# Selective scan and attention, two passes on one core: VectorE's side jobs moved to other engines in the first pass, the rotation and the position terms rebuilt in the second

## What is computed

```python
x = x + _L0_conv_ref(_gn(x), ...)   # state-space block
x = x + _L1_conv_ref(_gn(x), ...)   # attention block

# _L0: xh, z = split(x @ in_proj_w.T); xc = silu(conv3x3(xh) + conv_b)
#      four directions k: dts, Bs, Cs from x_proj_w; dts = softplus(dts @ dt_projs_w + bias)
def step(h, inp):                    # 192 channels x 16 states x 4 directions, 1024 steps
    u_t, d_t, B_t, C_t = inp
    dA = jnp.exp(d_t[..., None] * As)
    h = h * dA + (d_t * u_t)[..., None] * B_t[:, :, None, :]
    y = jnp.einsum('bkcn,bkn->bkc', h, C_t)
#      y summed over directions, layer norm, times silu(z), @ out_proj_w.T

# _L1: q, k, v = x @ w_qkv + b; 12 heads of 32
def rot(t):                          # pairs (even, odd) turned by cos, sin of the position
    return stack([t0 * c - t1 * s, t0 * s + t1 * c], axis=-1)
attn = einsum(rot(q), rot(k)) * scale
attn = attn + rel_h[..., :, None] + rel_w[..., None, :]   # q times a table, by row and by column
out = softmax(attn) @ v @ w_proj + b_proj
```

## Time and profile before

| | us |
|---|---|
| median of 3 runs | 3307.79 |
| lowest, highest | 3305.24, 3314.67 |
| profiled execution, its own time | 3309.41 |
| span of that execution in the trace | 3307.6 |
| busy: TensorE, VectorE, ScalarE, GpSimd | 2748.0, 2366.0, 1557.4, 1335.6 |

### The profile page before, as it was taken

The page is one execution under the profiler, slowest core; times in us unless marked ns, Lnnn a source line. Parts: engine busy times, 40 slices in busy tenths (PEclk is TensorE's granted clock), DMA queues, the critical chain, the costliest instruction groups (busy, mean ns, idle before and its releaser), DMA issues. The chain is left out here.

```text
span 3307.6 us, 40573 instructions
## 1 busy us (share of the span) xinstructions
PE 2748.0 (83%) x15824; PEld 1382.7 (42%) x15824; DVE 2366.0 (72%) x2262; ACT 1557.4 (47%) x1908; POOL 1335.6 (40%) x636
## 2 busy tenths in 40 slices
PE   3577777887678876777667999989998999989999
PEld 1222223332233332222222665556554665555655
DVE  1598899999999999999982466625664356625665
ACT  4445644555435564444431356514563346514564
POOL 4478766887668876766651100011000200011000
PEclk8789998999999999999896999999999999999999
DMA  1334443355443544445541111020111110020110
GB/s 61 128 115 133 153 144 141 130 140 159 145 149 127 140 159 145 161 134 144 182 137 60 30 33 52 1 71 1 33 52 40 33 33 25 29 71 1 33 52 20
DMA packets 93429, 297.51 MB, mean 90 GB/s; under 512 B 15804, under 2 KB 18504, under 8 KB 93224
## 3 DMA queue, kind: packets, MB, share of 16 engines
q1 hardware_dynamic: 93224, 294.73, 28.6%
HBM read 238.57 MB, written 23.07 MB: 79 GB/s over the span
## 5 line engine op out<-in xcount | busy, mean ns | idle before, releaser
L1608 POOL TENSOR_TENSOR arena<-arena 128x1024 f32<-128x1024 f32 x384 | 902.9, 2365 | 325.9 <-DVE arena L1092 277.3
L1092 DVE TENSOR_TENSOR_SCAN arena<-PS,arena 128x1024 f32<-128x1024 f32 x384 | 878.2, 2287 | 86.1 <-ACT PS L1445 62.5
L1445 ACT ACTIVATE PS<-arena,a_inf,a_neg 128x1024 f32<-128x1024 f32 x384 | 463.8, 1208 | 776.8 <-DVE arena L1092 772.4
L564 PE MATMUL PS<-arena,ident 128*128 128x512 f32 x1568 | 804.1, 639 | 19.3 <-ACT arena L1456 15.1
L1225 DVE CUSTOM_DVE_ANT_1 arena<-PS,arena 128x1024 f32<-128x1024 f32 x384 | 467.6, 1219 | 350.4 <-PE PS L851 350.4
L1533 ACT ACTIVATE arena<-arena,neg_max 128x1024 f32<-128x1024 f32 x384 | 441.0, 1149 | 513.4 <-DVE neg_max L1225 513.4
L555 PE MATMUL PS<-arena,sel 96*128 96x512 bf16 x768 | 247.7, 406 | 413.0 <-DVE arena L1100 409.3
L1100 DVE TENSOR_TENSOR arena<-arena,PS 128x1024 f32<-128x1024 f32 x384 | 459.3, 1196 | 9.7 <-PE PS L555 8.9
L564 PEld LDWEIGHTS PS<-arena,ident 128*128 128x128 f32 x1568 | 318.5, 204 | 304.2 <-issue 246.9
L851 PE MATMUL PS<-arena 64*128 64x512 f32 x1536 | 433.1, 641 | 11.1 <-DMA arena<-arena 11.1
L862 PE MATMUL PS<-ident,arena 128*128 128x128 f32 x3072 | 413.9, 278 | 2.6 <-ACT arena L1533 2.6
(11 more groups left out here) (125 smaller groups left out, 2286.2 us busy)
## 6 DMA issues: line engine op xcount, KB each, us to landing
arena<-b_rows SPq DMA_DIRECT2D x256, 512.0 KB, 3.7
arena<-b_rows SPq DMA_DIRECT2D x256, 256.0 KB, 4.0
arena<-arena SPq DMA_DIRECT2D x192, 128.0 KB, 2.9
arena<-arena SPq DMA_DIRECT2D x120, 64.0 KB, 2.0
normed<-xn SPq DMA_DIRECT2D x5, 1536.0 KB, 6.4
normed<-x_in SPq DMA_DIRECT2D x4, 1536.0 KB, 7.9
residual<-x_in SPq DMA_DIRECT2D x4, 1536.0 KB, 8.0
x<-residual SPq DMA_DIRECT2D x4, 1536.0 KB, 6.4
```

What stands on the lines that cost most here:

```text
L564: last = pe.matmul(dst[:, half(h)], lhs, rhs[:, half(h)], start=start, stop=stop, skip_group_check=True)
L1092: dve.tensor_tensor_scan(HS[:, at % 2, ::step], DA[:, ::step], DBU[:, at % R3, ::step], 0.0, ALU.mult, ALU.add).then_inc(scan_done.sem, 1)
L1445: act.activation(DA, DELTA[:, tile % 2, :], ACT.Exp, bias=a_inf[:, col:col + 1], scale=a_neg[:, col:col + 1]).then_inc(da_ready.sem, 1)
L1608: pool.tensor_tensor(DBU[:, at % R3, :], DU[:, tile % 2, :], BSB[:, at % R3, :], ALU.mult).then_inc(dbu_ready.sem, 1)
```

## The change

First pass. The statistics, their moments, both norms, the addition of x, the mask and the split into bfloat16 parts leave VectorE. ScalarE takes the sums (activations with an accumulated output), the norms, the mask (one Relu into bytes; the activation `soft_third` goes), the casts; GpSimd takes small products and the two subtractions of the split; TensorE adds x by a third product with the identity. The next image's statistics and norm move into the previous image's items (negative places), many jobs are placed anew, and the first image's front products run on VectorE instead of GpSimd.

Second pass. The weights' columns are ordered so that a head's even and odd parts lie 64 rows apart: the rotation is two VectorE products from swapped halves, without `turn`. A head's rows are then gathered by 10 DMAs instead of 6. The row term comes out of `relh`, 16 products with 32-column weights per job, already by query; the column term takes the one-hot rows. `relw` and half of `rel` go.

```diff
-HEAD_DMAS = 6
+HEAD_DMAS = 10
-PE_MID = {("y", 0, 0): 7, ("y", 0, 1): 8, ("y", 0, 2): 9, ... ("out", 0): 42, ("out", 1): 43, ("out", 2): 44,
-          ("out", 3): 45, ("out", 4): 46, ("out", 5): 47, ("stats",): 53}
+PE_FRONT = {("stats",): -8, ("xh", 0): 5, ("xh", 1): 6, ("xh", 2): 7, ("pad", 0): 25.5, ("pad", 1): 26, ("pad", 2): 27,
+            ("z", 0, 0): 56, ("z", 0, 1): 57, ("z", 0, 2): 58, ("z", 1, 0): 61, ("z", 1, 1): 62, ("z", 1, 2): 63,
+            ("dts", 0): 70, ("dts", 1): 71, ("dts", 2): 72, ("bc", 0): 75, ("bc", 1): 76, ("bc", 2): 77}
+PE_MID = {("y", 0, 0): 9, ("y", 0, 1): 10, ("y", 0, 2): 11, ("y", 1, 0): 13, ("y", 1, 1): 14, ("mean", 0): 21,
+          ("mean", 1): 22, ("var", 0): 30, ("var", 1): 31, ("out", 0): 43, ("out", 1): 44, ("out", 2): 45,
+          ("out", 3): 46, ("out", 4): 47, ("out", 5): 48, ("stats",): 53}
-DVE_MID = {... ("add", 0): 44, ("add", 1): 45, ("add", 2): 46, ...
+DVE_MID = {("centre", 0): 24, ("centre", 1): 25, ("scale", 0): 34, ("scale", 1): 34.5}
+ACT_FRONT = {("stat", 0, 0): -20, ("stat", 0, 1): -19, ("stat", 1, 0): -18, ("stat", 1, 1): -15, ("stat", 2, 0): -14,
+             ("stat", 2, 1): -11, ("means",): -6, ("rstd",): -4, ("norm", 0): -3, ("norm", 1): -2, ("norm", 2): -1,
+             ("xh",): 8, ("pad",): 28, ("z", 0): 59.5, ("z", 1): 64.5,
+             ...
+             ("ucopy", 3): 69, ("dts",): 73.5, ("brows",): 79, ("bchi",): 80, ("bmid",): 83, ("blo",): 86}
+ACT_MID = {("yf", 0): 12, ("yf", 1): 16, ("sq", 0): 27, ("sq", 1): 28.5, ("rstd",): 33, ("affine", 0): 35.5,
+           ("affine", 1): 37, ("out", 0): 43.9, ("out", 1): 44.9, ("out", 2): 45.9, ("out", 3): 46.9, ("out", 4): 47.9,
+           ("out", 5): 48.9, ("means",): 54.9, ("rstd2",): 56, ("norm", 0): 58.9, ("norm", 1): 60.5, ("norm", 2): 61}
+POOL_FRONT = {("var",): -5.5, ("bias",): -3.5, ... ("rest", 0): 81.5, ("rest", 1): 85}
+def front_due(table, b, i):
...
+            item = at + ITEMS * (f - b - 1)
+            if f == 1 and at < 0:
+                item = (at + EARLY) * 0.2
...
                     half_product(banks(k % 2, 1), h, [
                         (W["w_out"][:, 0, c * P:(c + 1) * P], flat(yf(m, 0))),
-                        (W["w_out"][0:XT, 1, c * P:(c + 1) * P], flat(yf(m, 1)[0:XT, :]))]).then_inc(op_psum.sem, 1)
+                        (W["w_out"][0:XT, 1, c * P:(c + 1) * P], flat(yf(m, 1)[0:XT, :])),
+                        (idn, flat(X[:, c, :]))]).then_inc(op_psum.sem, 1)
...
+                elif what == "out":
+                    k, = args
+                    h, c = divmod(k, CT)
+                    act.wait_ge(op_psum.sem, op_psum.at(2 * CT * m + k + 1))
+                    act.activation(X[:, c, half(h)], banks(k % 2, 1), ACT.Copy, accum_out=half_sums[:, h, c, 0:1])
+                    act.activation(banks(k % 2, 1), banks(k % 2, 1), ACT.Square, scale=1.0 / IMG,
+                                   accum_out=half_sums[:, h, c, 1:2]).then_inc(x_saved.sem, 1)
...
+            def small_mask(tile):
+                act.activation(MASK, SE, ACT.Relu, bias=mask_top[:, 0:1], scale=-MASK_TOP / SMALL
+                               ).then_inc(soft_mask.sem, 1)
...
             def soft_series(tile):
-                dve.wait_ge(soft_e.sem, soft_e.at(tile + 1))
-                dve.tensor_scalar(MASK, SE, SMALL, None, ALU.is_lt)
                 dve.wait_ge(soft_q2.sem, soft_q2.at(tile + 1))
-                dve.scalar_tensor_tensor(out=SQ3, in0=SQ3, scalar=2.4375, in1=SE, op0=ALU.add,
+                dve.scalar_tensor_tensor(out=SQ3, in0=SQ3, scalar=0.8125, in1=SE, op0=ALU.add,
                                          op1=ALU.mult).then_inc(soft_q.sem, 1)
...
+        JOBS = [[("proj", n) for n in range(4)] + [("rel", 0), ("rel", 1), ("relh", 0), ("relh", 1)],
+                [("proj", n) for n in range(4, 10)] + [("rel", n) for n in range(2, 6)]
+                + [("relh", n) for n in range(2, 6)],
+                [("proj", 10), ("proj", 11)]]
+        JOB_AT = [{k: m for m, k in enumerate([2, 4, 6, 8, 10, 12, 16, 18, 20, 22, 24, 25, 26, 27])}, {6: 0, 10: 1}, {}]
...
+                    copies = [[], [], [(QX[2 * HD * h + HD:2 * HD * h + 2 * HD, j, :], RELC[j::HG, g // 2, :])
+                                       for h in range(2)]]
+                    for h in range(2):
+                        for odd in range(2):
+                            at = XT * odd + HALF_HEAD * j
+                            rows = slice(2 * HD * h + HALF_HEAD * odd, 2 * HD * h + HALF_HEAD * (odd + 1))
+                            copies[0].append((QX[rows, j, :], QKC[at:at + HALF_HEAD, PLACE[g, "q"], :]))
+                            copies[1].append((KX[rows, j, :], QKC[at:at + HALF_HEAD, PLACE[g, "k"], half(h)]))
...
+                        for r in range(IMG // 2):
+                            at = h * IMG // 2 + r
+                            t, row = divmod(r, HG)
+                            last = pe.matmul(dst[IMG * row:IMG * row + IMG, t * P:(t + 1) * P],
+                                             QKC[:, PLACE[g, "q"], at * IMG:(at + 1) * IMG],
+                                             W["rel_h"][:, 0, HG * (IMG - 1 - at):HG * (REL - at)],
+                                             start=True, stop=True, skip_group_check=True)
...
-                        dve.tensor_tensor(RT2[:, h, :], src, W["sin"][:, 0, half(h)], ALU.mult
+                        dve.tensor_tensor(RT2[0:XT, h, :], raw[XT:P, :], W["sin"][XT:P, 0, half(h)], ALU.mult)
+                        dve.tensor_tensor(RT2[XT:P, h, :], raw[0:XT, :], W["sin"][0:XT, 0, half(h)], ALU.mult
                                           ).then_inc(sin_done.sem, 1)
```

More of the change, by code:

```diff
@@ L49 @@
[L49 to L60, removed]
@@ L73, in due @@
-def due(table, i):
-    return sorted((job for job, at in table.items() if i <= at < i + 1), key=table.get)
+            POOL_FRONT[("add", _m, _j)] = _b
+SIG_ORDER = sorted(range(4), key=lambda which: ACT_FRONT[("sig", which, 0)])
+SIG_DONE = sorted(range(4), key=lambda which: ACT_FRONT[("sig", which, 2)])
+CAP_ORDER = sorted(range(4), key=lambda which: POOL_FRONT[("cap", which)])
+SP_FRONT = {("next_x",): 72, ("z_store",): 80, ("b_store",): 83, ("bcs",): 89}
+SP_MID = {("x_load",): 1, ("z_load",): 2, ("x1_store",): 52, ("xn2_store",): 67}
@@ L78, in in_order, with mid_due @@
 def in_order(table):
     return sorted(table, key=table.get)
+def front_due(table, b, i):
+    found = []
+    for job, at in table.items():
+        for f in (b + 1, b + 2):
+            item = at + ITEMS * (f - b - 1)
+            if f == 1 and at < 0:
+                item = (at + EARLY) * 0.2
+            if f < B and i <= item < i + 1:
+                found.append((item, f, job))
+    return [(f, job) for item, f, job in sorted(found, key=lambda found: found[0])]
+def mid_due(table, b, i):
+    return sorted((job for job, at in table.items() if b and i <= at < i + 1), key=table.get)
@@ L521, in _ @@
                         sp.wait_ge(s_psum.sem, s_psum.after(b, STEPS * g - HG + j + 1))
-                        for dst, src in operands(g, j):
+                        for dst, src in itertools.chain(*operands(g, j)):
                             sp.dma_start(dst, src).then_inc(head_loaded[j].sem, 16)
@@ L786, in value_product @@
                         last.then_inc(v_psum.sem, 1)
-                job_saved = {"proj": raw_saved, "turn": sin_done, "rel": rel_saved, "relw": relw_saved}
+                job_saved = {"proj": raw_saved, "rel": rel_saved, "relh": relh_saved}
                 def job(phase, m, blocks=()):
@@ L1101, in times_c @@
                                   ).then_inc(hc_ready.sem, 1)
-            for job in in_order(DVE_FRONT):
-                front(0, *job)
+            for job in in_order(POOL_FRONT):
+                if job[0] not in ("var", "bias"):
+                    front_products(dve, 0, *job)
             dve.wait_ge(consts.sem, consts.at(N_CONST))
@@ L1238, in _ @@
                     biased_scores(s)
-                    if k - 2 in JOB_AT[g]:
-                        job(g + 1, JOB_AT[g][k - 2])
+                    for after, kinds in ((4, ("proj",)), (2, ("rel", "relh"))):
+                        if k - after in JOB_AT[g] and JOBS[g + 1][JOB_AT[g][k - after]][0] in kinds:
+                            job(g + 1, JOB_AT[g][k - after])
                     if g + 1 == GROUPS and k - 2 in LATE_AT:
@@ L1705 @@
     mats["w_out"] = wo
-    mats["w_qkv"] = np.asarray(L1_conv_w_qkv)
+    pos = np.arange(P)
+    paired = HD * (pos % XT // HALF_HEAD) + 2 * (pos % HALF_HEAD) + pos // XT
+    qkv_order = np.arange(3 * C)
+    for k in range(2 * GROUPS):
+        qkv_order[k * P:(k + 1) * P] = k * P + paired
+    mats["w_qkv"] = np.asarray(L1_conv_w_qkv)[:, qkv_order]
     mats["w_proj"] = np.asarray(L1_conv_w_proj)
@@ L1718 @@
     mats["to_high"] = np.eye(P, k=XT)
-    turn = np.zeros((P, P), f)
-    for i in range(0, P, 2):
-        turn[i + 1, i] = -1.0
-        turn[i, i + 1] = 1.0
```

(1 more changed line is left out.)

544 lines of the change are left out of this document (258 added, 286 removed).

## The result

The changed kernel takes 3465.68 us (median of 4 runs, 3463.32 to 3467.5) against 3308.34 for the kernel before (the three runs of its table and a fourth): ratio 1.0473, 95% interval 1.0456 to 1.0489. It is slower by 157 us; the prediction said 3472, +164.

A forecast was written before the change was run, and what follows sets the result against it. VectorE, with ScalarE close behind, bounds the loop and TensorE the second pass. Terms -1 ahead, +137 loop, +12 behind, +16 second pass give +164 on 3309.4, 3473; median 3472 us, range 3380 to 3540.

The forecast's parts named there:

- The deciding step: First-pass loop: ScalarE's output jobs share TensorE's item, stretching 18 scans; 144 us plus 36 for the clock, together 180.
- The other waits at one item's distance: First-pass loop: other ScalarE jobs one item behind TensorE, plus the second image's early norm, cost 55 us, from 30 to 75.
- The gain: First-pass loop: VectorE loses 117 us of instructions, less 14 for waits for decay and overlap, so 103 us gained.
- The term of +12: Behind the loop: twelve more output product records at 1.2 GHz cost 12 us, or 5 at full clock.
- The change of head group: Second pass: 40 DMAs instead of 24 make the chain 10.1 us longer, all exposed, twice an image; clock 1.5 each.
- The side jobs: Second pass: TensorE's work beside the steps shrinks by 10.7 us an image.
- Rival B: Second pass: 16-row DMA issues cost only 0.42 us each; total 3415 us; chance 0.17.
- Rival C: Second pass: `relh` does not overlap its four column groups, 3.5 us a job; total 3532 us; chance 0.06.
- A (TensorE ahead of ScalarE): First-pass loop: TensorE reaches output products before ScalarE does, so the 180 us disappear; total 3292 us; chance 0.13.
- E (clock up in the gaps): First-pass loop: TensorE's clock stays up in the gaps; total 3436 us, inside the forecast's spread; chance 0.56 together with the forecast.
- Rival D: Both passes: VectorE's freed time all returned, 144 us in the loop and 85 behind it; total 3078 us; chance 0.03.
- the signs named beforehand: Included scans 11 to 15 us apart in items 43 to 48, VectorE below 80%, score waits about 10 us.

The follow-up runs named there:

- the run with two items' distance: Changed kernel with ScalarE's six output jobs per image two items behind TensorE's products instead of in the same item: 3310.23 us, ratio 0.9995.
- the run with the mask alone: Kernel before with only the series' mask made by ScalarE and the third folded into ScalarE's Square: 3300.73 us, ratio 0.9972.
- the version with the orders mended: Changed kernel, output and other ScalarE jobs two items behind, some GpSimd products moved, ScalarE issuing k's copies, taps' additions put back: 3160.96 us, ratio 0.9541.

## Why the prediction was right, step by step

**The deciding step** was the order: a ScalarE job in the item of TensorE's product costs the whole way from scan to product. Predicted: 11.6 us between scans at full clock, 13.6 with the clock; measured 11.19 for the first of six, where the item work still ran at 2.4 GHz, and 12.9 to 13.6 for the others, in each of three images. Predicted sum 180, measured 170 above 3.57 (9.4 each, 18 times); the run with two items' distance gives back 155 of the 157 us. Inside the term three sizes were off and partly cancelled: ScalarE's two activations and their reads take 1.19 us (714.06 to 715.25), not 1.75; the output product takes 3.13 (710.89 to 714.02), not 2.75; TensorE's item work took 3.9 us at 1.2 GHz instead of 2.25, so 1.7 for the clock where 2.0 was taken. That sums to 12.97, where the prediction's terms give 13.6.

**The other waits at one item's distance.** Predicted 55 with the early norm of the second image. Read off as what the items show above their former length: item 12 +12 in three images, item 28 +8, item 54 +9, item 59 +7, item 64 +6; with items 1 to 3 for the early norm, +10 above 3.57 (6.5 above their former length), 52. Not foreseen were items 15 and 16 (5.36 and 4.32 us), behind the second product for y, which TensorE reached late and began at 1.2 GHz: 8 us in all. Moving ScalarE's jobs one item on gave 43 us back.

**The gain.** 117 us of VectorE's instructions were to go. Summed one by one they fell from 1568.4 to 1450.7, 118 less; but neighbours had overlapped by 53.9 us and now overlap by 37.6, so the busy time fell by 101 only. The prediction had put 14 against the 117 for this and for the waits for decay; with stalls of 170 + 52 + 8 and a loop of +142, what is left for it is 30. That is a remainder and not a measurement: items 65, 90, 33, 52, 25, 4 and 58, in none of the lists, grew by another 22.6 us in all, and counted as stalls they leave only 7. Two of them are waits for GpSimd: after item 65 the scan came 1.61 us late behind its product (4.3 us over the images), and in item 90 the pick took 3.12 us (3.7 in all). Inside the 118, L1073 was missed (it waits for GpSimd too, 1.57 instead of 1.30 us, 6 more), and mask and series together fell by 84.8 - 63.2 = 21.6 here, 15.3 in the run with the mask alone. The prediction's 15.9, with the wait passed on, stands; 57 would have been the naive count. The Trainium skill (SBUF — State Buffer, Who interferes with whom) states that a VectorE instruction with two SBUF inputs contends with a GpSimd instruction that reads SBUF, and that whichever was issued first holds the shared ports while the other waits. The waiting agrees with this case, 4.83 us against 1.22 with GpSimd idle; the order agrees only for GpSimd's first product, for VectorE's multiplication also waited through the second, which began after it.

**Loop:** predicted +137, measured +142: the large stall 10 us smaller, the other waits 3 smaller, 8 not foreseen, and the rest, 10 us more, between a smaller gain and the items in none of the lists (GpSimd's 5 among them, 8 by the two items above). That the two numbers lie within 5 us is partly luck.

**Ahead and behind.** -1 predicted, -2.8 measured. Behind the loop +12 predicted, -2.1 measured. The step that failed is the clock: the earlier trace rows had the products at 1.2 GHz throughout, and I let that stand. In the changed kernel it rose while they ran:

```profile
1905.94 4.07 PE L617 MATMUL PS<-arena,w_out 128*128 128x512 f32 x4 [9.53 <-POOL arena L1607]
...
1911.81 3.91 PE L617 MATMUL PS<-arena,w_out 128*128 128x512 f32 x4
...
1917.52 2.76 PE L617 MATMUL PS<-arena,w_out 128*128 128x512 f32 x4
...
1921.17 2.07 PE L617 MATMUL PS<-arena,w_out 128*128 128x512 f32 x4
```

Four records fell from 4.07 to 2.07 us with TensorE busy without a gap since 1905.94, so that 36 records took 24.3 us, as long as the 24 before. The term of +12 was therefore nothing; the 2.1 us less came behind the products, where the statistics take 4.9 us instead of 7.0. These 14 us are the largest miss of the sum, and with the loop's 5 us the other way they leave the forecast 10 us above the trace's +154.

**Second pass.** Predicted +16, measured +16.7 in the trace and +13.9 alone. Its terms: up to the first step -8.4, measured -8.8 (1935.09 to 1974.95, 39.9 us, where the kernel before took 48.65; -8.2 as the mean of four images). The change of head group +10.1 and 1.5 for the clock, measured 46.75 - 34.7 = +12.1. The side jobs -10.7: 96 steps grew by 12.4 us, less 2 x 12.1 for the changes, so -11.8. Rival B (cheap 16-row copies) is out by the 27.00 us for 40. The waits at a change, in the changed kernel:

```profile
2466.48 2.08 PE L920 MATMUL PS<-arena 64*128 64x512 f32 x4 [3.44 <-DMA arena<-arena]
...
2473.02 1.13 PE L920 MATMUL PS<-arena 64*128 64x512 f32 x4 [0.87 <-DMA arena<-arena]
...
2479.24 2.08 PE L920 MATMUL PS<-arena 64*128 64x512 f32 x4 [4.06 <-DMA arena<-arena]
```

3.44, 0.87 and 4.06 us for three of the heads, 8.4 together, with TensorE back at 1.2 GHz behind the long ones (2.08 instead of 1.13). Rival C (no overlap in `relh`) is out by this row, 32 records in 1.08 us:

```profile
2449.71 1.08 PE L883 MATMUL PS<-arena 128*32 128x128 f32 x32
```

Rivals A (TensorE ahead of ScalarE) and E (clock up in the gaps) are out by the timeline of the item at 703.51. Rival D, everything returned, would be 3078; the version with the orders mended reaches 3161. TensorE full in items 46 to 50 (about 23 us in three images, 5 x 1.55 each) and the waits for GpSimd are parts of the difference that the runs name.

Of the signs named beforehand all came but one, by a hair: VectorE is 81% busy in the loop, not below 80; the wait of the scores at a change is 8.4 us, near the 10.

## What to carry to other kernels

Before work is moved to an engine that runs its jobs in a fixed order, read from the trace when the producer reaches its step and when the consumer reaches its own: the distance in items, not the work, set 198 of the 305 us between the changed kernel and the mended one. An instruction's mean in the profile is not its price if it waits for another engine: look at one instance with that engine idle (0.69 us for the mask, where the mean was 2.47), and expect the next two-input instruction to inherit the wait. The copies at a change of head group cost their issues, 0.67 us each with 16 rows or 32; count issues for each queue before halving their rows, and give part of them to a queue whose engine has room.

## What was not expected of the hardware

A VectorE multiplication with two SBUF inputs waited through two products of GpSimd, the second of which began 1.4 us after it had itself begun (679.51, 680.92, end 684.3): it did not get its turn between them. TensorE's clock behaved in two ways: behind an idle 9.53 us it stayed at 1.2 GHz through some 13 us of float32 products without a gap and rose inside their row (in the kernel before, behind 9.52, through all 24 us); in items 44 to 48, behind an idle 5.9, the granted clock was at 2.4 again 3.6 to 4.9 us after TensorE had resumed, in or just ahead of the output product. Why the two differ no run here settles. Copies from SBUF to SBUF took ScalarE's queue 1.17 and 1.53 us for two, close to SyncE's 0.67 each, and the exponent between them kept its 1.15 us.
